# Moving a projection piece and half of a projection between steps of a hand-ordered attention kernel

## The reference

```
q = x @ Wq + bq;  k = ctx @ Wk + bk;  v = ctx @ Wv + bv
attn = softmax(q k^T * scale + mask);  x = layernorm((attn v) @ Wo + bo + x)
```

```
s = k_t v_t + w_t * s;  out_t = r_t (u k_t v_t + s)         # per head, over the tokens
x1 = x + (groupnorm(out) * silu(xg @ Wg.T)) @ Wo.T
xc = layernorm(x1);  y = x1 + sigmoid(xr2 @ Wfr.T) * (square(relu(xk2 @ Wfk.T)) @ Wfv.T)
```

## Time and profile before

| | us |
|---|---|
| median of 3 runs | 1161.53 (1160.98 to 1165.46) |
| the profiled execution, its own time | 1163.91 |
| its span in the trace | 1162.1 |
| PE busy | 1041.7 (90%) |
| ACT busy | 862.3 (74%) |
| DVE busy | 588.2 (51%) |
| POOL busy | 320.6 (28%) |

### The profile page before, as it was taken

One profiled execution on the slowest core, in us unless ns is written; L12 is line 12 of the kernel. 1 busy time (PEld: TensorE's weight loads), 2 busy tenths in 40 slices (PEclk: granted clock), 3 DMA queues, 4 the chain that ended last, 5 costly groups with the idle time before them and its releaser, 6 DMA issues.

```text
span 1162.1 us, 17967 instructions
## 1 busy us (share of the span) xinstructions
PE 1041.7 (90%) x7026; PEld 356.1 (31%) x7026; DVE 588.2 (51%) x948; ACT 862.3 (74%) x947; POOL 320.6 (28%) x359
## 2 busy tenths in 40 slices
PE   3298989999999999999999999999998999878866
PEld 2031223323333233323332333323331233214413
DVE  5040116555647365754655564736575364545373
ACT  2279888888888888888888888888888888880110
POOL 3670061233214131415123321414141002400320
PEclk8599999999999999999999999999999999988676
DMA  4946024722545233803472254523260045000400
GB/s 143 220 125 153 9 83 98 151 31 71 119 71 116 72 80 65 159 7 90 101 147 35 72 119 71 115 73 72 66 101 16 7 101 79 5 14 14 58 16 12
DMA packets 68876, 91.65 MB, mean 79 GB/s; under 512 B 9664, under 2 KB 49648, under 8 KB 68784
## 3 DMA queue, kind: packets, MB, share of 16 engines
q1 hardware_dynamic: 64608, 85.25, 33.3%
q0 software_dynamic: 2480, 4.12, 1.8%
q10 hardware_dynamic: 1696, 1.06, 0.4%
HBM read 50.74 MB, written 18.62 MB: 60 GB/s over the span
## 4 chain that ended last, share of the span: by engine, by line
PE 56%; ACT 17%; issue 14%; DVE 6%; DMA 3%; POOL 2%; ACTq 1%; SPq 0%; POOLq 0%; DVEq 0%
PE psum L861 55%; ACT probs L775 14%; DVE vs L1428 1%; DMA vs<-v_c 1%; ACT L832 1%; POOL xm L609 1%; ACT L775 1%; ACTq L299 1%; POOL vs L632 1%; POOL vs L623 1%; DMA q_stack<-q_stacked 1%; PE psum L951 1%; ACT xm L832 0%; ACT xm L829 0%; PE psum L882 0%
## 5 line engine op out<-in xcount | busy, mean ns | idle before, releaser
L775 ACT ACTIVATE probs<-psum 128x1024 f32<-128x1024 f32 (+1 forms) x832 | 798.5, 1022 | 184.8 <-PE psum L861 182.2
L861 PE MATMUL psum<-probs,v_aug 128*9 128x512 f32 (+1 forms) x3328 | 425.9, 603 | 1.3 <-DVE o_raw L1352 1.2
L861 PE MATMUL psum<-q_stack,k_stack 64*128 64x512 bf16 (+1 forms) x1750 | 323.6, 392 | 58.6 <-ACT probs L775 44.6
L861 PEld LDWEIGHTS psum<-q_stack,k_stack 64*128 64x128 bf16 (+1 forms) x1750 | 84.2, 95 | 476.9 <-ACT probs L775 384.4
L1435 DVE TENSOR_TENSOR_SCAN vs<-w_c,vs 128x514 f32<-128x514 f32 x64 | 102.6, 1602 | 21.6 <-POOL vs L623 17.0
L632 POOL TENSOR_TENSOR vs<-r_c,vs 128x512 f32<-128x512 f32 x64 | 86.5, 1361 | 95.5 <-DVE tmp L1412 53.9
L609 POOL TENSOR_TENSOR xm<-tmp,xa 128x512 f32<-128x512 f32 x40 | 45.5, 1156 | 226.4 <-DVE tmp L1404 226.4
L861 PEld LDWEIGHTS psum<-probs,v_aug 128*9 128x9 f32 (+1 forms) x3328 | 58.4, 89 | 149.3 <-issue 141.3
L1352 DVE COPY o_raw<-psum 128x512 f32<-128x512 f32 x32 | 22.1, 691 | 111.6 <-PE psum L861 111.6
L596 POOL TENSOR_TENSOR rstd<-moments,eps 128x2 f32<-128x2 f32 x24 | 4.7, 197 | 237.8 <-DVE moments L1370 237.8
L1404 DVE SCALAR_TENSOR_TENSOR tmp<-psum,chan,sx 128x256 f32<-128x256 f32 x80 | 33.7, 478 | 59.7 <-PE psum L861 58.8
(11 more groups left out here) (181 smaller groups left out, 1023.9 us busy)
## 6 DMA issues: line engine op xcount, KB each, us to landing
vs<-v_c SPq DMA_DIRECT2D x61, 257.0 KB, 7.3
ctx_t<-in_mask SPq DMA_DIRECT2D x8, 1601.0 KB, 6.6
k_stacked<-k_parts SPq DMA_DIRECT2D x48, 200.1 KB
ctx_t<-in_ctx_t SPq DMA_DIRECT2D x24, 400.0 KB, 6.3
k_stack<-k_stacked SPq DMA_DIRECT2D x31, 300.2 KB, 6.4
q_stack<-q_stacked SPq DMA_DIRECT2D x31, 192.0 KB, 6.8
q_stacked<-q_parts SPq DMA_DIRECT2D x88, 64.0 KB, 3.3
ctx_t<-in_ctx_t SPq DMA_DIRECT2D x8, 401.0 KB, 6.4
```

The costliest lines, as they stand in the source:

```text
L775: nc.scalar.activation(probs[turn_step % NP][t][0:w, :, :], ps[t][0:w, :, :], ACT.Exp).then_inc(exped.sem, 1)
L861: return nc.tensor.matmul(dst, lhsT, rhs, start=start, stop=stop)
```

## The change

Four edits. Piece 3 of the key/value projection moves from step 42 to step 40, right behind piece 2, into the same bank 7 as before and with the same wait. The first half of the queries' projection moves from step 46 to step 42, the second stays at step 46, and both go into bank 5 in place of bank 7; the first half waits for the square root's read of bank 5 (`std_ready`). Step 42 joins `LIGHT`, in all turns. On DVE the bias of piece 3 is done right behind that of piece 2, before the chain that ends in `og_ready`, in place of behind it. The turning of `xn` into bank 7 waits for the last bias in place of the queries' scaling.

```diff
-LIGHT = (2, 4, 8, 10, 12, 20, 24, 26, 28, 38, 48, 50)
+LIGHT = (2, 4, 8, 10, 12, 20, 24, 26, 28, 38, 42, 48, 50)
...
-KV_STEP = [30, 32, 40, 42]
+KV_STEP = [30, 32, 40, 40]
...
-            def project_q(a, to):
+            def project_q(a, to, parts=range(EC)):
                 pe.wait_ge(xt_in.sem, xt_in.at(a))
-                for m in range(EC):
+                for m in parts:
...
                     elif step == 48:
                         pe.wait_ge(xn2_ready.sem, xn2_ready.at(c))
                         if f is not None:
-                            pe.wait_ge(q_scaled.sem, q_scaled.at(f))
+                            pe.wait_ge(kv_biased.sem, kv_biased.at(f))
...
-                    if step == 46:
-                        pe.wait_ge(kv_biased.sem, kv_biased.at(f))
-                        project_q(f, 7)
+                    if step == 42:
+                        if c is not None:
+                            pe.wait_ge(std_ready.sem, std_ready.at(c))
+                        else:
+                            pe.wait_ge(kv_biased.sem, kv_biased.at(f, 2))
+                        project_q(f, 5, (0,))
+                    elif step == 46:
+                        project_q(f, 5, (1,))
...
                     if f is not None:
                         bias_kv(f, 2, KV_BANK[2])
+                        bias_kv(f, 3, KV_BANK[3])
...
-                    if f is not None:
-                        bias_kv(f, 3, KV_BANK[3])
...
-                        scale_q(f, 7)
+                        scale_q(f, 5)
```

## The result

| | before | after |
|---|---|---|
| median of 20 runs each, us | 1161.67 (1158.51 to 1166.74) | 1154.8 (1150.55 to 1162.95) |
| ratio after / before | | 0.9943, 95% interval 0.9927 to 0.9958 |
| the profiled execution, its own time | 1163.91 | 1153.55 |
| its span, PE's mean clock | 1162.1, 0.949 | 1151.7, 0.954 |

The kernel is faster by 4.9 to 8.5 us, 6.9 by the medians.

The account below looks back on a forecast made before the run. Neither PE nor ACT alone bounds the kernel; they hand the time to each other. Terms 7.5 + 1.6 + 0.0 + 1.6 = 10.7 took the profiled 1163.91 to 1153.2; adjusted to the runs' median, the forecast was 1152.3, range 1148.5 to 1157.5.

Parts of the forecast that it names:

- Piece 3 into PE's wait at step 40: Step 40, turns with c and f: piece 3's 1.54 us fill PE's wait of 1.43 before (42,0); 0.1 is left over.
- Light at step 42 and half a projection: Steps 42 to 48: (43,0) follows without a gap, Wo starts 0.75 earlier, gain 1.26 at (48,0) and 1.50 at (48,1).
- The same collision of xn goes away: DVE before step 48: xn's scalings, 2.06 us beside POOL's cast, would end before it begins; worth nothing by itself.
- Steps 48 to 51 are ACT's in both versions: End of a turn: ACT sets the pace in steps 48 to 51 before and after, so the 1.5 us gain stays.
- Five turns at 1.5: Turns 1 to 5, which have c and f: each gains 1.5 us, bounds 0 and 1.7, together 7.5.
- Turns 6 and 7 at 0.8: Turns without piece or projection: the light order alone removes most of the gap before (43,0), 0.8 us each, 1.6 together.
- Turn 0 at 0.0: Turn 0, where step 40 hides nothing: piece 3's 1.54 us offset by 0.55 and 1.0; bounds -0.5 and +0.5.
- The clock, 1.6: Turn 5, before (43,0): with PE's step 40 wait filled, the clock's fall should go, 1.6 us, bounds 0 and 1.6.
- A: Rival, step 44: piece 3's bias and the cast delay the gate, Wo waits; 1157.4, or 1159.9 with all gain gone; 12%.
- B: Rival, turns 6 and 7: shifted by some 9 us, one or both clock falls do not come; 1148.1 to 1150.2; 11%.
- C: Rival, DVE: the reciprocal is stretched beside POOL's cast, Wo starts 3.8 late, 2.3 us a turn lost, 1171.4; 4%.
- D: Rival, steps 42 and 43: PE's scores wait more often and the clock falls there, 1.6 us a turn, 1160.3; 3%.

## Why the prediction was right, and where it was off

**The sign and the place were right; the time lay 2.5 above the forecast of 1152.3 and inside the range.** 6.9 were measured where 9.2 had been forecast. By steps:

**Piece 3 into PE's wait at step 40: right.** A pair lasts 2.95 (3.1 was said), weigh 39 starts 2.89 behind the pair's start (3.08 was reckoned), PE's wait of 1.43 is gone, (42,1) does not wait. What the forecast did not say is that this is worth nothing by itself (0.00): with the half moved beside it it is worth 0.67 (from +0.34 to -0.33), without the light order. With the light order alone beside it, it was not measured.

**Light at step 42 and half a projection: right down to (48,1), and a little better than forecast.** The forecast was worked out on turn 4, which it took to be like the others "to a few hundredths"; it is 0.28 late at (44,0). In turns 1 to 3 and 5, (44,0) stands 6.08 behind (41,0) (6.03 was forecast), Wo at 8.50 in place of 9.33 (8.58). (48,0) wins 1.46 and (48,1) 1.69, against the 1.26 and 1.50 of the forecast: with (47,0) moved by Wo's 0.75, its (48,0) is some 1.96 behind (47,0), where two tiles without a gap are 1.83 from start to start; the 1.94 of a row is from the first one's start to the second one's end. In turn 4 the two win 1.30 and 1.53. ACT's wait before (44,0) is 0.42 (0.69 in turn 4) and not 0.2 to 0.3, as the tiles in front of it end sooner than reckoned.

**"The same collision of xn goes away": this step failed.** It grew, from 2.06 to 2.92. The forecast moved `xn` by 1.6 and POOL's cast by 0.75 and found them apart; it left out that `k_rest`, which stands in front of the cast, holds DVE as well. In the profile of before, the first scaling began at 658.97, only 0.33 before `k_rest` ended, and took 0.48 where a free one takes 0.40; the earlier trace rows do not have the row:

```profile
656.07 3.23 POOL L572 TENSOR_TENSOR k_rest<-kv,k_parts 64x1601 f32<-64x1601 f32 x1
```

Moved earlier, it is held for all of its overlap. The end of `xn` hangs on POOL's chain, which moved only as Wo did (0.66 in turn 4, 0.83 in the others, counted from (41,0)), and not on the queries' scaling. With it fell "Steps 48 to 51 are ACT's in both versions": PE waits 0.44 for `xn`, ACT 0.42 before (50,0), and of the 1.69 won at (48,1) 1.15 are left at the next turn. Moving POOL's work away gave 1.66 a turn: shown by two kernels, one that frees `xn` at no price (-0.51) and one that frees it and holds the gate's chain instead (-0.25). So the forecast's 1.5 was a sum of two errors of opposite sign: 0.16 too little for the order, and nothing for the hold, which takes 0.51.

By the Trainium skill (SBUF — State Buffer, "SBUF: two separate sides") the lock between DVE and POOL lasts for the whole instruction. The holds of this case agree: each held instruction ends 0.15 to 0.55 after one of POOL's. The forecast should have laid each one of POOL's against each of DVE's, `k_rest` too.

**Five turns at 1.5: off by 0.35 each** (0.52 in turn 4), 5.6 for 7.5. **Turns 6 and 7 at 0.8: right** (0.82 and 0.80, the falls in both). **Turn 0 at 0.0: right** (24.94 and 24.94).

**The clock, 1.6: not shown.** The fall in turn 5 went, as forecast (27.35 to 24.55), but in the same profile one stands at step 15 of turn 3 that costs as much. PE there, and ACT behind it:

```profile
450.84 1.89 PE L860 MATMUL psum<-probs,v_aug 128*9 128x512 f32 x8
```

```profile
453.38 1.94 ACT L774 ACTIVATE probs<-psum 128x1024 f32<-128x1024 f32 x2 [1.84 <-PE psum L860]
```

In turn 2 the same wait of ACT is 0.77:

```profile
327.53 1.94 ACT L774 ACTIVATE probs<-psum 128x1024 f32<-128x1024 f32 x2 [0.77 <-PE psum L860]
```

Nor does the fall in turn 5 hang on PE's wait at step 40 alone: the kernels with only the half moved and with only the light order keep that wait of 1.43, and have no fall there (26.05 and 25.36 in turn 5, as in their turns 1 to 3). So the term belongs to the single execution and was not shown to belong to the kernel. Of the 10.4 between the two profiled executions, 7.2 are the order (5.6 and 2 x 0.8); the other 3.2 are the falls of the clock in turns 5 and 3 and behind turn 7, the start and the 0.6 of turn 0. The medians differ by 6.9, and 7.2 lies inside both intervals (4.9 to 8.5, 4.5 to 10.5). A forecast of 5.6 + 1.6 without a clock term, from 1161.53, would have been 1154.3.

**Rivals.** A did not happen: the gate ends 6.17 after (41,0), 2.5 before Wo. It becomes true with `k_rest` beside the gate's chain, at 0.27 a turn. B did not show in the profile of the change, but did for turn 7 in its profile of the five rounds; with the three products neither turn has a fall. C fell: the reciprocal beside the cast takes 3.34, the same as alone, and is not even held. It began before the cast, but the kernel before has the other order, which the forecast could have looked at: five times a reciprocal of the same size begins while POOL is in a product, and takes 3.34 too.

```profile
672.78 1.27 POOL L604 TENSOR_TENSOR x_rows<-x_rows,rows 128x512 f32<-128x512 f32 x1
673.42 3.34 DVE L1357 RECIPROCAL den_t<-den_t 128x512 f32<-128x512 f32 x1
```
D fell: no fall at steps 42 and 43 of turns 1 to 5 in either profile of the change.

**Open:** what makes the clock fall at step 15, where PE's rows ahead of it in turn 3 are those of turn 2; the 0.6 in the first steps of turn 0; the late (44,0) of turn 4; and whether filling the waits of turns 6 and 7 only moves the falls, to step 34 and to the end. To take the waits at step 15 away was not tried.

## What to carry to other kernels

When an edit moves a DVE instruction, lay every POOL instruction near its new place against it, and ask what the end of the held one releases: a hold that cost 0.1 us before (0.48 for 0.40) can cost 0.9 after (1.34) and be the next wait. Edits that each remove one wait of a loop between two engines do not add up; price them together, at the last landmark that both engines share, and go on to the end of the turn. A fall of the clock in one profile may be a property of that execution: keep it out of the sum unless several profiles have it at the same step. And take sizes from several turns: one turn of five was 0.17 off here.

## What the runs showed of the hardware that was not expected

- A DVE scaling of f32 from SBUF to SBUF (128 x 256, 0.73 for two when free) that starts beside a POOL product or cast ends 0.15 after that one ends: 1.35 and 1.65 long in the change. A two-input DVE product (128 x 512) is held in the same way, 2.15 long for 0.69 beside `k_rest`, and ends 0.55 after it; POOL's cast, which begins before that end, takes 1.86 for 1.51. A reciprocal of that size is not held: 3.34 beside a cast of 1.52, 3.34 beside `k_rest`, 3.34 begun within a POOL product, and 3.34 alone.
- The clock fell to 1.2 GHz also at step 15, at a price of 1.5 to 1.6, where PE's last wait is 0.53 and the same in turns without a fall: in one or two of turns 1 to 6 in seven of the thirteen profiles, and in different turns from one to the next.
- With three products nobody reads in a wait of 2.84 us, PE stayed at 2.4 GHz behind it and the stretch was 2.2 us shorter; in turn 7 it was as short in two profiles without them. The whole time gained 2.5 by the medians, within the intervals.
- The same kernel, profiled twice, took 110.5 and 115.3 us behind its last exponential, by where the clock fell.
- One execution of the light order ran at a granted clock of 0.85 where the others have 1.00 (0.826 in the mean instead of about 0.95), and took 1230 us; it was not seen again.
